# A recurrence, layer norms and a top-2 mixture of experts on one core: VectorE's order in the routing stage is rearranged, with TensorE's fillers and ScalarE's roots

## The chip, the cores and the metric

The kernel runs on one core of one Trainium2 chip. The metric is the device time of one execution in microseconds, lower is better. The kernel before takes 311.33 us (median of three runs, 310.96 to 311.38).

## What is computed

The input is 8 steps of 512 tokens with 128 features each. An LSTM runs over the 8 steps; its output is added to the input and normalised. Then the 4096 tokens go, in 8 groups of 512, through a mixture of 8 experts with two experts a token and 128 places an expert and group, and a second layer norm follows. Cut to what matters:

```python
def step(carry, xp_t):                       # x_proj = x @ w + bias, for 8 steps of 512 rows
    h_prev, c_prev = carry
    g = xp_t + h_prev @ u                    # [512, 4*128]
    gates = sigmoid(g[:, :3 * H]); c_cand = tanh(g[:, 3 * H:])
    c = fg * c_prev + ig * c_cand            # ig, fg, og = gates
    h = og * tanh(c)
    return (h, c), h
x = layernorm(x + lstm(x))
raw = softmax(einsum('GSM,ME->GSE', x, router_w))     # G = 8 groups of S = 512, E = 8
idx1 = argmax(raw); idx2 = argmax(raw without idx1)   # m1, m2: one hot; gate1, gate2
p1 = cumsum(m1) - m1;  p2 = cumsum(m2) - m2 + m1_count     # place in the expert; dropped if >= C = 128
expert_inputs = einsum('GSEC,GSM->EGCM', dispatch, x)
hidden = gelu(expert_inputs @ w0[e]) * (expert_inputs @ w1[e])     # 128 -> 680
out = einsum('EGCM,GSEC->GSM', hidden @ wo[e], combine)
x = layernorm(x + out)
```

## The kernel before

**Stages.** The loop over s (0 to 7) is the recurrence. Features lie on the partitions, 512 tokens in the columns. Products by w and by the experts' weights are made of three products of high and low parts (fp32r): ScalarE copies the high part, VectorE subtracts the low part (`low_x` for inputs, `low_weights` for a quarter of an expert, the low part of what follows). The h product is fp32. Behind the loop comes the expert stage: units u of one expert and two groups (later four), each with six chunks k; `first(u, k)` makes two products, ScalarE the gelu, VectorE `chunk` the product of both and `low_hid` its low part, and `second(u, k)` the output product three chunks later. The last stage is the second layer norm and the stores.

**One step s.** TensorE (L586 to L595): `h_part(s)` waits for h(s-1) and adds h @ u to four banks `big[0..3]`; `turn_sum(s-1)` transposes x + h into `b_ht` or `b_xnt`; `logits(s-1)` makes the router's products; `x_part(s+1)` fills the banks for the next step; `places(b)` counts for a batch b of two steps (`chosen` in, counts in `b_xt` out). ScalarE (L726 to L744): four Tanh of the gates, `exp(b)` of the softmax between gate 1 and gate 2, `norm_rows(s-2)` in two halves around the Tanh of the cell, then high parts by the lists `HIGH_X` and `HIGH_BY_ACT`. VectorE (L980 to L1031), in this order: `sum_y(s-1)` (x + h), `best(s-2)` (top two of the logits), `shift(s-2)` (the norm's offset, waits for GpSimd's root), `scale_less(b)` in odd steps; the first two parts of `assign_batch` in even steps; `term_f`; the softmax and the choice (`gate_step` 0 to 3) in odd steps, or the rest of `assign_batch` in even ones; `term_i`; `gate_step` 4 (`chosen`); the cell; `slot_base`; `stat(s-1)`; h; then moments and variance, `gate_values` and `gate_row` in odd steps, and `low_weights` by the list `LOW_BY_STEP`. The batch b = s // 2 - 1 is chosen in the odd step s, and its assignment (`slot_ix`, where each token's row goes) is made in the even step behind it.

**GpSimd** runs one queue in order (L479 to L489): `power(s)` is the norm's root x ** -0.5 of step s, and `scatter(b, ...)` issues two indirect DMAs for each of 8 tiles of 128 tokens, which write the normalised rows with their token number and gates to `slots`. It waits for `slot_step` (the assignment) and for `gate_rows_in`. Roots 3 to 7 stand among the scatters, ahead of the tile that `ROOTS_AMONG` names. `power(s)` also waits for the rows of step s-2. Behind the 64 scatters come the adds of the experts' output. **SyncE** loads and stores in order: `load_expert(e)` waits until the low parts of expert e-2 are made; `load_xd(u)` waits for the 16 scatters of its batches.

**Entering the expert stage.** `turn_xd(0)` transposes the first rows into `big[3]`, ScalarE and VectorE split them (`high_xd`, `low_xd`), and `first(0, 0)` starts. Batch 2's assignment, step 7's norm and batch 3's whole routing are still to do; VectorE does them between the chunks of units 0 to 3 (L1147 to L1193), among them `shift(S - 1)`, which waits for root 7, ahead of `chunk(0, 5)`.

**The last stage.** ScalarE copies the last outputs (`copy_y`, `last_y`), writes five early rows (`LATE_ROWS`), and then for each of two pairs of groups takes a square root (`fin_sqrt`, L812) and writes rows (L819). VectorE adds the last sums (`fin_add`, L1203), makes statistics (L1211), moments (L1215), the argument (L1221), and five small steps from the square root to scale and offset (`fin_root_step`, L1232 to L1241).

## Time and profile before

| | us |
|---|---|
| median of the runs (310.96 to 311.38) | 311.33 |
| the profiled execution's own time | 310.78 |
| its span, first to last instruction | 309.0 |
| busy in the span: TensorE, VectorE, ScalarE, GpSimd | 279.8, 257.9, 213.5, 176.7 |
| recurrence, until the last h product's start | 63.5 |
| first product of the expert stage | 74.0 |
| mean granted clock of TensorE | 0.979 of 2.4 GHz |

A row of a timeline gives the start in us, the duration, engine, line of the kernel, operation, what is written and read, its shape, how many instructions are merged in it, and in brackets the time for which the engine was idle before it, with what ended that. Instructions of one engine overlap a little, so in a full queue starts stand closer than durations.

### The profile page before, as it was taken

How to read it: one execution, taken by the hardware profiler on the slowest of the kernel's cores; microseconds unless marked ns; L12 is line 12 of the kernel's file. 1: busy time of each engine (PE TensorE's matmuls, PEld its weight loads, DVE VectorE, ACT ScalarE, POOL GpSimd, SP SyncE). 2: the span in 40 equal slices, each digit the busy share in tenths (PEclk: the TensorE clock that was granted, in tenths of full speed). 3: DMA queues.
4: the chain of work that ended last, by engine and by line, in shares of the span. 5: the costliest groups of instructions: out<-in, count | busy, mean ns of one | idle time of the engine just before them, and what ended most of it. 6: DMA issues, size and time to landing. Idle time of an engine off the chain costs nothing.

```text
span 309.0 us, 5728 instructions
## 1 busy us (share of the span) xinstructions
PE 279.8 (91%) x1671; PEld 233.7 (76%) x1671; DVE 257.9 (83%) x816; ACT 213.5 (69%) x484; POOL 176.7 (57%) x148
## 2 busy tenths in 40 slices
PE   8999988975969999999999999999999999897840
PEld 8666555635968999999998787788888888787730
DVE  2789997899859998888888988988777678899975
ACT  4787865556687777776778687776655665564964
POOL 5011148878777787776878578827447265662400
PEclk9999999977999999999999999999999999999995
DMA  6996081724273227224454857524223135452444
GB/s 193 379 395 238 8 253 48 217 69 134 78 225 92 71 69 228 65 57 52 72 93 35 204 71 164 71 20 64 45 25 45 26 34 146 67 94 19 79 143 136
DMA packets 46109, 34.97 MB, mean 113 GB/s; under 512 B 6993, under 2 KB 40720, under 8 KB 46080
## 3 DMA queue, kind: packets, MB, share of 16 engines
q1 hardware_dynamic: 35392, 26.56, 28.9%
q0 software_dynamic: 10688, 8.07, 17.8%
q8 instruction: 13, 0.21, 0.3%
q14 instruction: 16, 0.13, 0.1%
HBM read 17.86 MB, written 17.10 MB: 113 GB/s over the span
## 4 chain that ended last, share of the span: by engine, by line
PE 60%; DVE 15%; issue 8%; ACT 8%; POOL 8%; POOLq 0%; ACTq 0%; DVEq 0%
PE big L617 10%; PE big L619 10%; PE big L618 10%; POOL slots L464 6%; PE b_xnt L633 3%; PE b_xnt L636 3%; PE b_xnt L634 3%; PE big L531 2%; PE b_ht L633 2%; PE b_ht L636 2%; PE b_ht L634 2%; PE b_rt L653 2%; PE b_ht L578 2%; DVE e_lo L977 2%; PE b_xt L573 2%
## 5 line engine op out<-in xcount | busy, mean ns | idle before, releaser
L791 ACT ACTIVATE act_g<-big 128x256 f32<-128x256 f32 (+1 forms) x144 | 65.1, 452 | 55.4 <-PE big L619 54.6
L617 PE MATMUL big<-x_hi,e_hi 128*128 128x256 f32 (+1 forms) x264 | 84.7, 321 | 1.2 <-DVE x_lo L1037 1.2
L618 PE MATMUL big<-x_hi,e_lo 128*128 128x256 f32 (+1 forms) x264 | 84.4, 320 | 0.0
L619 PE MATMUL big<-x_lo,e_hi 128*128 128x256 f32 (+1 forms) x264 | 84.4, 320 | 0.0
L464 POOL DMA_INDIRECT slots<-rows,slot_ix x64 | 66.9, 1046 | 24.1 <-issue 18.4
L474 POOL DMA_INDIRECT tokens<-contrib,token_ix x32 | 50.3, 1572 | 32.0 <-DVE token_ix L1063 17.0
L474 POOL DMA_INDIRECT tokens<-zero_rows,token_ix x28 | 44.9, 1603 | 27.1 <-DVE token_ix L1063 20.0
L617 PEld LDWEIGHTS big<-x_hi,e_hi 128*128 128x128 f32 x264 | 50.2, 190 | 5.2 <-issue 1.5
L619 PEld LDWEIGHTS big<-x_lo,e_hi 128*128 128x128 f32 x264 | 50.3, 191 | 3.9
L618 PEld LDWEIGHTS big<-x_hi,e_lo 128*128 128x128 f32 x264 | 50.1, 190 | 3.9
L531 PE MATMUL big<-h,u_half 128*128 128x512 f32 x56 | 27.3, 633 | 3.5 <-DVE h L1018 3.5
L731 ACT ACTIVATE act_g<-big,bias_g 128x512 f32<-128x512 f32 x31 | 20.8, 685 | 8.1 <-PE big L531 7.7
L453 POOL TENSOR_TENSOR root_y<-root_x,minus_half 128x4 f32<-128x4 f32 x8 | 9.8, 1220 | 28.7 <-DVE root_x L882 28.7
L1071 DVE TENSOR_TENSOR term_i<-act_g,big 128x256 f32<-128x256 f32 (+3 forms) x36 | 18.3, 508 | 8.7 <-PE big L619 4.5
L1071 DVE TENSOR_TENSOR cell<-act_g,big 128x256 f32<-128x256 f32 (+1 forms) x36 | 18.3, 507 | 7.9 <-ACT act_g L791 4.4
L1071 DVE TENSOR_TENSOR h<-act_g,big 128x256 f32<-128x256 f32 (+3 forms) x36 | 18.3, 509 | 7.5 <-PE big L619 4.5
L531 PEld LDWEIGHTS big<-h,u_half 128*128 128x128 f32 x56 | 10.9, 200 | 16.7 <-issue 11.2
L977 DVE TENSOR_TENSOR e_lo<-e_raw,e_hi 128x544 fp32r<-128x544 f32 x32 | 22.6, 718 | 0.1
L1071 DVE TENSOR_TENSOR term_f<-act_g,big 128x256 f32<-128x256 f32 (+1 forms) x36 | 18.3, 507 | 5.1 <-PE big L619 2.9
L712 ACT ACTIVATE e_hi<-e_raw 128x544 fp32r<-128x544 f32 x32 | 20.1, 649 | 0.0
L756 ACT ACTIVATE hid_hi<-term_f 128x256 fp32r<-128x256 f32 (+1 forms) x36 | 17.3, 481 | 2.6 <-DVE term_f L1071 2.3
L756 ACT ACTIVATE h_hi<-h 128x256 fp32r<-128x256 f32 (+3 forms) x36 | 17.3, 481 | 1.6 <-DVE h L1071 1.5
(207 smaller groups left out, 654.1 us busy)
## 6 DMA issues: line engine op xcount, KB each, us to landing
e_raw<-in_L_ffn_w_kernel_dram SPq DMA_DIRECT2D x16, 320.0 KB
slots<-zero_rows SPq DMA_DIRECT2D x8, 548.0 KB, 8.4
e_raw<-in_L_ffn_wo_kernel_dram SPq DMA_DIRECT2D x8, 320.0 KB
xd<-slots SPq DMA_DIRECT2D x16, 137.0 KB, 2.5
xd<-slots SPq DMA_DIRECT2D x8, 274.0 KB, 3.1
x<-in_L_attn_input_seq_dram SPq DMA_DIRECT2D x8, 256.0 KB, 4.5
tokens<-rows SPq DMA_DIRECT2D x8, 256.0 KB, 2.7
x<-tokens SPq DMA_DIRECT2D x8, 256.0 KB, 3.2
```

What stands on the lines that cost most here:

```text
L464: pool.indirect_dma_start(slots, bass.IndirectOffsetOnAxis(ap=slot_ix[b][:, 2 * t + c:2 * t + c + 1], axis=0), rows[:, b * BT + t, :], Non ...
L474: pool.indirect_dma_start(tokens, bass.IndirectOffsetOnAxis(ap=tokens_of(u)[:, k:k + 1], axis=0), contrib(u)[:, k, :], None, bounds_check= ...
L531: pe.matmul(big[k][:, :], u_half[:, g * D:(g + 1) * D], h2[:, :], start=False, stop=True).then_inc(gate_ready, 1)
L617: pe.matmul(dst, e_hi[q][:, c0:c0 + m], xdt_hi[u % 2][:, 0:w], start=True, stop=False)
L618: pe.matmul(dst, e_lo[q][:, c0:c0 + m], xdt_hi[u % 2][:, 0:w], start=False, stop=False)
L619: mm = pe.matmul(dst, e_hi[q][:, c0:c0 + m], xdt_lo[u % 2][:, 0:w], start=False, stop=True)
L712: nc.scalar.activation(e_hi[e % RING_E][:, piece(n)], e_raw[e % 2][:, piece(n)], ACT.Copy).then_inc(ehi_ready[e % RING_E], 1)
L731: nc.scalar.activation(act_g[k][:, :], big[k][:, :], ACT.Tanh, bias=bias_g[:, gate_order[k]:gate_order[k] + 1], scale=1.0 if k == 2 else 0 ...
L756: nc.scalar.activation(hid_hi[n % RH][0:m, 0:width(u)], hid[n % RH][0:m, 0:width(u)], ACT.Copy).then_inc(hidhi_ready, 1)
L791: nc.scalar.activation(act0[n % RH][0:m, 0:w], pre(n, P)[0], ACT.Gelu_apprx_tanh).then_inc(gelu_ready, 1)
L977: dve.tensor_tensor(e_lo[e % RING_E][:, piece(n)], e_raw[e % 2][:, piece(n)], e_hi[e % RING_E][:, piece(n)], ALU.subtract).then_inc(elo_re ...
L1071: dve.tensor_tensor(hid[n % RH][0:m, 0:w], act0[n % RH][0:m, 0:w], pre(n, P)[1], ALU.mult).then_inc(hid_ready, 1)
```

## The change

VectorE makes `term_f` ahead of `shift` and `scale_less`, and `term_i` and the cell ahead of the whole softmax and choice (`gate_step` 0 to 4). Behind h, in the same odd step, it makes `void_base` (split off `gate_values`), all six parts of the batch's assignment, `gate_values` and `gate_row`; in the last step only `void_base`, since batch 2's assignment stays behind the loop, with its `gate_values` and `gate_row`. The low parts are spread anew: four quarters in step 2 (two of them ahead of `term_i`), one in step 3 (ahead), two in step 4, none in step 5, two in step 6; three of expert 2 come behind the loop instead of two. ScalarE makes `exp` behind all four gates and takes four high parts of expert 2 to other places, three of them ahead of `norm_rows`. Roots 5 to 7 move two scatters back on GpSimd. TensorE makes `logits(s-1)` in even steps between the halves of `x_part`, and dummy products (`keep_warm`) are added: ten behind step 6, twelve before `turn_xd(0)` and ten behind it. In the last stage ScalarE makes a dummy square root ahead of the last `copy_y`, the first real one comes after two of the five late rows, and VectorE makes its five steps of the first root ahead of `fin_add(0)`.

```diff
--- before.py
+++ after.py
@@ -48,9 +48,11 @@
     RING_E = 4
     HIGH_X = {0: [2, 3], 1: [4, 5], 2: [6, 7]}
     LOW_X = {0: [2, 3], 1: [4, 5], 2: [6, 7]}
-    HIGH_BY_ACT = {1: [(0, 0), (0, 1), (0, 2)], 2: [(0, 3), (1, 0)], 3: [(1, 1), (1, 2), (1, 3)], 4: [(2, 0), (2, 1)], 5: [(2, 2), (2, 3)]}
-    LOW_BY_STEP = {s: [((s - 2) // 2, 2 * (s % 2) + n) for n in range(2)] for s in range(2, 7)}
-    ROOTS_AMONG = {(0, 2): 3, (0, 5): 4, (0, 7): 5, (1, 2): 6, (1, 5): 7}
+    HIGH_BY_ACT = {1: [(0, 0), (0, 1), (0, 2)], 2: [(0, 3), (1, 0)], 3: [(1, 1), (1, 2), (1, 3)], 5: [(2, 2)]}
+    HIGH_AHEAD = {4: [(2, 0), (2, 1)], 6: [(2, 3)]}
+    LOW_AHEAD = {2: [(0, 0), (0, 1)], 3: [(1, 0)]}
+    LOW_BY_STEP = {2: [(0, 2), (0, 3)], 4: [(1, 1), (1, 2)], 6: [(1, 3), (2, 0)]}
+    ROOTS_AMONG = {(0, 2): 3, (0, 5): 4, (1, 0): 5, (1, 3): 6, (1, 6): 7}
     HIGH_AT = {3: [(3, 1), (3, 4), (4, 1), (4, 4)], 4: [(11, 4), (11, 5), (12, 2), (12, 3)], 5: [(12, 4), (12, 5), (13, 2), (13, 3)],
                6: [(13, 4), (13, 5), (14, 2), (14, 3)], 7: [(14, 4), (14, 5), (15, 2), (15, 3)]}
     LOAD_AT = {0: 4, 5: 5, 13: 6, 14: 7}
@@ -573,12 +575,12 @@
                     mm = pe.transpose(b_xd(u)[:, k * P:(k + 1) * P], xd[u % 4][:, k, 0:D], ident[:, :])
                 mm.then_inc(xdt_ready, 1)
 
-            def keep_warm(n):
+            def keep_warm(n, home):
                 for _ in range(n):
-                    pe.matmul(b_ht[:, 0:P], ones[:, :], ones[:, :], start=True, stop=True)
+                    pe.matmul(home[:, 0:P], ones[:, :], ones[:, :], start=True, stop=True)
 
             pe.wait_ge(pool_consts, 1)
-            keep_warm(12)
+            keep_warm(12, b_ht)
             x_part_0()
             router_sums()
             x_part(1, range(4))
@@ -586,14 +588,23 @@
             for s in range(1, S):
                 h_part(s)
                 turn_sum(s - 1)
-                logits(s - 1)
+                if s % 2 == 1:
+                    logits(s - 1)
                 if s + 1 < S:
                     x_part(s + 1, range(0, 2))
+                if s % 2 == 0:
+                    logits(s - 1)
+                if s + 1 < S:
+                    x_part(s + 1, range(2, 4))
                 if s >= 3 and s % 2 == 1:
                     places(s // 2 - 1)
-                if s + 1 < S:
-                    x_part(s + 1, range(2, 4))
+                if s == S - 2:
+                    pe.wait_ge(slot_step, AS * (GB - 1) + 2)
+                    keep_warm(10, b_xt)
+            pe.wait_ge(gate_read, gate_no(S - 1, 2))
+            keep_warm(12, big[2])
             turn_xd(0)
+            keep_warm(10, big[2])
 
 
             def first(u, k):
@@ -730,8 +741,10 @@
                     act.wait_ge(gate_ready, gate_no(s, k))
                     nc.scalar.activation(act_g[k][:, :], big[k][:, :], ACT.Tanh, bias=bias_g[:, gate_order[k]:gate_order[k] + 1],
                                          scale=1.0 if k == 2 else 0.5).then_inc(gate_read, 1)
-                    if k == 1 and s >= 3 and s % 2 == 1:
-                        exp(s // 2 - 1)
+                if s >= 3 and s % 2 == 1:
+                    exp(s // 2 - 1)
+                for e, n in HIGH_AHEAD.get(s, []):
+                    high_weights(e, n)
                 if s >= 2:
                     norm_rows(s - 2, range(0, 2))
                 act.wait_ge(cell_ready, s + 1)
@@ -803,6 +816,7 @@
                     for n in EARLY_ROWS.get((u - NU, k), []):
                         early_row(n)
             high_hid(NU - 1, NCH - 1)
+            nc.scalar.activation(root_p[:, 0, 0:1], eps[:, :], ACT.Sqrt)
             copy_y(NU - 1)
 
 
@@ -820,12 +834,16 @@
                                              bias=root_b[:, 1, n:n + 1], scale=root_y[:, 1, n:n + 1]).then_inc(fin_ready[g], 1)
 
             last_y()
-            for n in LATE_ROWS:
+            for n in LATE_ROWS[:2]:
                 early_row(n)
-            for i in range(NB // 2):
-                fin_sqrt(i)
-                for g in range(HALF + GB * i, HALF + GB * (i + 1)):
-                    fin_rows(g)
+            fin_sqrt(0)
+            for n in LATE_ROWS[2:]:
+                early_row(n)
+            for g in range(HALF, LAST):
+                fin_rows(g)
+            fin_sqrt(1)
+            for g in range(LAST, S):
+                fin_rows(g)
 
         @block.vector
         def _(dve):
@@ -936,10 +954,13 @@
                                          op0=ALU.mult, op1=ALU.add).then_inc(base_step, 1)
                 dve.tensor_scalar(void[:, :, :], gates[:, :, :], 0.0, FAR, ALU.is_equal, ALU.mult).then_inc(base_step, 1)
 
-            def gate_values(b):
+            def void_base(b):
 
                 dve.wait_ge(base_step, 3 * b + 2)
                 dve.tensor_tensor(base[:, :, :], base[:, :, :], void[:, :, :], ALU.add).then_inc(base_step, 1)
+
+            def gate_values(b):
+
                 dve.wait_ge(chosen_ready, b + 1)
                 dve.tensor_tensor(gate_rows[:, :, :, :], chosen[:, :, :, :], gates[:, :, :].unsqueeze(3).broadcast_to([P, BT, 2, E]),
                                   ALU.mult).then_inc(gates_step, 1)
@@ -978,39 +999,34 @@
                                   ALU.subtract).then_inc(elo_ready, 1)
 
             for s in range(S):
-                odd, even = (s // 2 - 1 if s % 2 == 1 and s >= 3 else None), (s // 2 - 2 if s % 2 == 0 and s >= 4 else None)
+                b = s // 2 - 1
+                routes = s >= 3 and s % 2 == 1
                 if s >= 1:
                     sum_y(s - 1)
                 if s >= 2:
                     best(s - 2)
-                    shift(s - 2)
-                if odd is not None:
-                    scale_less(odd)
-                if even is not None:
-                    assign_batch(even, 0)
-                    assign_batch(even, 1)
                 if s >= 1:
                     dve.wait_ge(gate_read, gate_no(s, 0))
                     dve.scalar_tensor_tensor(out=term_f[:, :], in0=act_g[0][:, :], scalar=1.0, in1=cell2[:, :],
                                              op0=ALU.add, op1=ALU.mult).then_inc(terms_ready, 1)
-                if odd is not None:
-                    for n in range(4):
-                        gate_step(odd, n)
-                if even is not None:
-                    for n in range(2, AS):
-                        assign_batch(even, n)
+                if s >= 2:
+                    shift(s - 2)
+                if routes:
+                    scale_less(b)
+                for e, n in LOW_AHEAD.get(s, []):
+                    low_weights(e, n)
                 dve.wait_ge(gate_read, gate_no(s, 2))
                 ins = dve.scalar_tensor_tensor(out=term_i[:, :] if s else cell2[:, :], in0=act_g[1][:, :], scalar=1.0,
                                                in1=act_g[2][:, :], op0=ALU.add, op1=ALU.mult)
                 ins.then_inc(terms_ready if s else cell_ready, 1)
-                if odd is not None:
-                    gate_step(odd, 4)
                 if s >= 1:
                     dve.wait_ge(terms_ready, 2 * s)
                     dve.scalar_tensor_tensor(out=cell2[:, :], in0=term_f[:, :], scalar=0.5, in1=term_i[:, :],
                                              op0=ALU.mult, op1=ALU.add).then_inc(cell_ready, 1)
-                if odd is not None:
-                    slot_base(odd)
+                if routes:
+                    for n in range(5):
+                        gate_step(b, n)
+                    slot_base(b)
                 if s >= 1:
                     stat(s - 1, range(T))
                 dve.wait_ge(tanh_ready, s + 1)
@@ -1024,9 +1040,13 @@
                 if s >= 1:
                     moment(s - 1)
                     variance(s - 1)
-                if odd is not None:
-                    gate_values(odd)
-                    gate_row(odd)
+                if routes:
+                    void_base(b)
+                    if s < S - 1:
+                        for n in range(AS):
+                            assign_batch(b, n)
+                        gate_values(b)
+                        gate_row(b)
                 for e, n in LOW_BY_STEP.get(s, []):
                     low_weights(e, n)
 
@@ -1150,11 +1170,13 @@
             assign_batch(NB - 2, 0)
             assign_batch(NB - 2, 1)
             shift(S - 2)
-            low_weights(2, 2)
+            gate_values(NB - 2)
+            gate_row(NB - 2)
+            low_weights(2, 1)
             chunk(0, 0)
             assign_batch(NB - 2, 2)
             chunk(0, 1)
-            low_weights(2, 3)
+            low_weights(2, 2)
             assign_batch(NB - 2, 3)
             stat(S - 1, range(0, 2))
             chunk(0, 2)
@@ -1167,6 +1189,7 @@
             assign_batch(NB - 2, 5)
             shift(S - 1)
             chunk(0, 5)
+            low_weights(2, 3)
             best(S - 1)
             for k in range(3):
                 chunk(1, k)
@@ -1181,6 +1204,7 @@
                 elif k == 3:
                     slot_base(NB - 1)
                 elif k == 4:
+                    void_base(NB - 1)
                     gate_values(NB - 1)
                 elif k == 5:
                     gate_row(NB - 1)
@@ -1258,13 +1282,12 @@
                 for t in range(T):
                     fin_moment(g * T + t)
             fin_argument(0)
+            for n in range(FT):
+                fin_root_step(0, n)
             for k in range(GB):
                 fin_add(k)
                 for t in range(T):
                     fin_stat(LAST + k, t)
-                if k == 0:
-                    for n in range(FT):
-                        fin_root_step(0, n)
             for n in range(LAST * T, S * T):
                 fin_moment(n)
             fin_argument(1)
```

## Rows read from the trace of the kernel before

**Rows 1.** The page, part 4: the chain that ended last, by engine.
```profile
PE 60%; DVE 15%; issue 8%; ACT 8%; POOL 8%; POOLq 0%; ACTq 0%; DVEq 0%
```
**Rows 2.** Windows: length, busy us of PE, PEld, DVE, ACT, POOL, then clock, DMA, GB/s.
```profile
64.00:66.00 2.00, 2.00 (x4) 0.75 (x3) 2.00 (x7) 0.69 (x1) 1.74 (x2) 0.50 0.56 166
...
120.00:128.00 8.00, 8.00 (x70) 7.96 (x70) 7.03 (x21) 5.71 (x18) 6.17 (x7) 1.00 0.41 123
```
**Rows 3.** Timeline of PE, the h products of steps 2, 3, 4 and 7.
```profile
18.84 3.60 PE L531 MATMUL big<-h,u_half 128*128 128x512 f32 x8
...
26.41 3.59 PE L531 MATMUL big<-h,u_half 128*128 128x512 f32 x8
...
35.08 3.70 PE L531 MATMUL big<-h,u_half 128*128 128x512 f32 x8 [0.22 <-DVE h L1018]
...
63.53 5.40 PE L531 MATMUL big<-h,u_half 128*128 128x512 f32 x8 [2.05 <-DVE h L1018]
```
**Rows 4.** Timeline of DVE, steps 3 and 4.
```profile
28.64 0.68 DVE L863 SCALAR_TENSOR_TENSOR yd<-h,x 128x512 f32<-128x512 f32 x1
...
34.35 0.67 DVE L1018 SCALAR_TENSOR_TENSOR h<-act_g,tanh_c 128x512 f32<-128x512 f32 x1
...
35.42 0.17 DVE L942 TENSOR_TENSOR base<-base,void 128x16 f32<-128x16 f32 x1
...
35.97 1.35 DVE L977 TENSOR_TENSOR e_lo<-e_raw,e_hi 128x544 fp32r<-128x544 f32 x2
...
39.00 0.17 DVE L950 TENSOR_SCALAR cnt<-b_xt 128x16 f32<-128x16 f32 x1
...
41.00 0.17 DVE L966 TENSOR_TENSOR slot_ix<-pos,over 128x16 uint32<-128x16 f32 x1
```
**Rows 5.** Timeline of POOL, scatters 1, 10 and 18, roots 5 and 7.
```profile
42.12 1.45 POOL L464 DMA_INDIRECT slots<-rows,slot_ix  x1 [5.46 <-DVE slot_ix L966]
...
56.39 0.97 POOL L464 DMA_INDIRECT slots<-rows,slot_ix  x1 [0.31 <-issue]
...
64.06 1.44 POOL L453 TENSOR_TENSOR root_y<-root_x,minus_half 128x4 f32<-128x4 f32 x1 [0.51 <-DVE root_x L882]
...
69.62 0.97 POOL L464 DMA_INDIRECT slots<-rows,slot_ix  x1 [0.30 <-issue]
...
82.47 1.04 POOL L453 TENSOR_TENSOR root_y<-root_x,minus_half 128x4 f32<-128x4 f32 x1 [0.40 <-DVE root_x L882]
```
**Rows 6.** Timelines of PE and DVE, entering the expert stage.
```profile
78.31 0.36 PE L617 MATMUL big<-x_hi,e_hi 128*128 128x256 f32 x1
...
83.55 0.16 DVE L888 SCALAR_TENSOR_TENSOR root_b<-moments,root_y 128x4 f32<-128x4 f32 x1 [0.24 <-POOL root_y L453]
...
86.64 0.36 PE L639 MATMUL b_ht<-hid_hi,e_lo 128*128 128x256 f32 x1 [0.99 <-DVE hid_hi L1045]
...
92.78 0.39 PE L633 MATMUL b_xnt<-hid_hi,e_hi 128*128 128x256 f32 x1 [1.54 <-ACT hid_hi L756]
```
**Rows 7.** Timelines of ACT and DVE, the last stage.
```profile
294.79 0.38 ACT L762 ACTIVATE tanh_c<-b_xnt 128x256 f32<-128x256 f32 x1 [1.40 <-PE b_xnt L640]
...
297.30 0.76 DVE L1203 TENSOR_TENSOR x<-b_rt,x 128x256 f32<-128x256 f32 x2 [0.90 <-PE b_rt L666]
...
298.07 1.28 ACT L812 ACT_TABLE_LOAD   x1
...
299.70 0.20 DVE L1232 RECIPROCAL root_y<-root_p 128x8 f32<-128x8 f32 x1 [0.87 <-ACT root_p L812]
...
300.63 0.75 DVE L1203 TENSOR_TENSOR x<-b_ht,x 128x256 f32<-128x256 f32 x2
...
300.74 2.80 ACT L819 ACTIVATE x<-x,root_b,root_y 128x128 f32<-128x128 f32 x7 [1.08 <-DVE root_b L1241]
...
302.74 0.17 DVE L1221 TENSOR_SCALAR root_x<-fin_mom 128x8 f32<-128x8 f32 x1
...
303.45 0.29 ACT L812 ACTIVATE root_p<-fin_mom,eps 128x8 f32<-128x8 f32 x1
```

## The prediction

> **What bounds the kernel now.** Read the shares of the chain first [rows 1]: TensorE owns 60% of the chain that ended last, VectorE 15%, GpSimd and ScalarE 8% each, and 8% is issue, most of it GpSimd's. So there are stages in which another engine sets the pace. Then the windows [rows 2]: from about 112 to 256 us TensorE has no gap (the window from 120 is 8.00 of 8.00), so whatever moves the start of this stage moves the end by as much, and nothing inside it is touched. What counts lies ahead of it and behind it.
>
> Ahead of it the timelines show a recurrence of eight steps. A step whose h product starts at 18.84 and whose successor starts at 26.41 costs TensorE 7.57 us of its own work; the next takes 8.67 us, to 35.08, and there TensorE waits for h [rows 3]. VectorE explains it: from sum_y(2) at 28.64 to h(3) at 34.35 it runs without a gap, and the assignment of batch 0, cnt at 39.00 to slot_ix at 41.00, stands in the next step with a gate term of 0.60 between its parts [rows 4]. GpSimd waits 5.46 us for that slot_ix, starts at 42.12 and is then full: a scatter takes 0.97 us and 0.30 us of issue, and root 7, behind 26 scatters and four roots, starts at 82.47 [rows 5]. VectorE waits for root 7 at 83.55 (0.24 us), and what it does next releases TensorE at 86.64, after 0.99 us idle [rows 6]. The chain of waits runs through just these: POOL from 43.87 on, root 7, VectorE, the product at 86.64. So the first half is bound by GpSimd's start, by the number of scatters ahead of root 7, and by what VectorE does between shift(7) and low_hid(0,5).
>
> At the end the last ScalarE table load stands at 298.07, VectorE waits 0.87 us for its root, and the second root waits at 303.45 until ScalarE has written seven rows, though VectorE had its argument at 302.74 [rows 7].
>
> **Part 1, steps 2 and 3: later h, earlier slots.** A low part costs 0.64 us (two in 1.35 us with their overlap, row 35.97 of [rows 4]; one more in a queue adds 0.64). Step 2 gets four in place of two. The two more can cost VectorE between 0 and 1.27 us; since one pair stands ahead of term_i, where VectorE waits for the third gate, I take 0.54. h(2) ends later by as much, while TensorE is in its own work until 26.4: hidden. But VectorE enters step 3 at 29.18 instead of 28.64. Step 3 to h took 5.71 us (28.64 to 34.35); it gets one low part more (0.64) and two waits of some 0.12 us each where a result is used at once, since chosen no longer fills the wait ahead of the cell. h(3) starts at 29.18 + 5.71 + 0.64 + 0.25 = 35.78 instead of 34.35, and h product 4 at 36.5 instead of 35.1: **this step loses 1.4 us**, TensorE idle for about 1.3 of it. From h to void_base it takes 1.07 us as before (34.35 to 35.42): 36.85, with the add itself 36.94. Then the assignment: 39.00 to 41.17 less 0.60 for the gate term is 1.57, and 0.10 for a wait that the term used to cover. slot_ix is there at 38.6 instead of 41.17. The gate rows now follow it (35.51 to 35.97: 0.46 us, end 39.1), and GpSimd waits for them too. From slot_ix's end to the first scatter the trace has 0.95 us [rows 4, 5]; so GpSimd starts at 40.0, **2.1 us earlier**. Bounds: 39.5 if the delay counts from slot_ix alone, 41.0 if VectorE pays the whole 1.27 in step 2 and waits a little more in step 3.
>
> **Part 2, GpSimd up to root 7.** The roots move from (0,7), (1,2), (1,5) to (1,0), (1,3), (1,6): root 7 stands behind 28 scatters, not 26. The sum: 82.47, less the start's 2.1, less the waits of 0.51 (root 5) and 0.40 (root 7) for VectorE's arguments, which come in time now, plus 2 x 1.28 = 2.57: **82.0 instead of 82.47**. Four roots stay four. Argument 7 is made behind chunk (0,3), at about 81.2, and so doesn't hold it. Ten scatters with root 3 among them, 42.12 to 56.39, take 14.27 us; eight slots of 1.28 and one of 2.23 with the root would be 12.47, so 1.8 us of lengthening lie there (the first takes 1.45 instead of 0.97) [rows 5]. I leave it where it is. Without it root 7 would be at 81.2 (its argument), with twice it at 83.8.
>
> **Part 3, steps 4 to 7.** Step 4 has no assignment in it any more and is TensorE's 7.6 us; the two copies ahead of the rows on ScalarE (1.2 us) delay tanh, but h still ends inside TensorE's work. Step 5 has VectorE's assignment behind h and not two low parts, which is hidden or even, and root 3, 2.1 us earlier, is no longer waited for; I take 8.3 us. Step 6 is again TensorE's, 7.6, but ten dummies follow: the h product's four products are 8 pieces of 512 columns in 3.59 us, so a dummy of 128 columns, two pieces, is 0.21 us, and ten are 2.1 [rows 3]. So the last h product starts at 62.3, not 63.53. Before, TensorE had idled 2.05 us ahead of it, the granted clock was 0.50 from 64 to 66 (the level of 1.2 GHz), and the product took 5.40 instead of 3.6 [rows 2, 3]. Now the dummies fill that gap; I expect 3.6. Then it waits from about 67.0 to 68.4 for chosen(2) (shift(5), ahead of scale_less, waits some 1 us for root 5, which two more scatters put at 64.0 to 65.4), then 12 dummies (2.6), the turn of xd (whose rows are no longer waited for: their last scatter is 4 us earlier), 10 dummies (2.1): first(0,0) at 73.9, and at 2.4 GHz first(0,2) at 76.4 instead of 78.31 [rows 6]: 1.9 us earlier. VectorE, with 0.46 us of gate rows more ahead of its first chunk and 0.2 of pieces, comes to shift(7) at 82.1 instead of 83.31 and **waits there for root 7 until 83.1**. The 1.9 us end here, and 1.0 us of slack is left for all of this part: it is free unless it slips by more.
>
> **Part 4, behind root 7.** shift(7) is 0.45 us earlier. Low part (2,3) now stands between chunk (0,5) and best(7): +0.64, less about 0.3 of small waits that vanish, since everything is ready. The product of 86.64, which waits for low_hid(0,5), comes **0.15 us earlier**. The wait of 1.54 us at 92.78 [rows 6] follows the same chain (copy, exp's two table loads), so it moves along. Scatters of batches 1 to 3 end about 2.7 us earlier, which nobody waits for.
>
> **Part 5, the tail.** ScalarE idles 1.40 us until 294.79 [rows 7]. The dummy root with its table load (1.28, row 298.07) and about 0.2 goes there: 293.39 + 1.48 = 294.87, so 0.1 us late. Three of the five early rows, at 0.40 each (seven in 2.80), go behind sqrt(0): it starts at 296.95 and is done at 297.25. VectorE's five steps (299.70 to 300.63) follow at once and push fin_add(0) from 297.30 to 298.2. From there the old spacing without the steps between: add and stats 0, 1.47 us (297.30 to 298.77), add and stats 1 with eight moments 2.11 (300.63 to 302.74): sqrt(1) at 301.8. ScalarE's three early rows and seven rows (2.80) end at 301.2, ahead of it. Before it was 303.45: **1.65 us earlier**, and all behind it is unchanged. If the joined order hid nothing but the table load, it would be 1.3; if the 0.1 is also absorbed, 1.8.
>
> ScalarE's page of the Trainium skill (ScalarE: Activation LUTs, What ACT_TABLE_LOAD costs) says a switch costs about 1.28 us of load and 1.38 us of drain. That speaks against the dummy root: it wouldn't fit into the idle time. The row of 298.07 with 1.28 and VectorE released at 299.70 by the root behind it leaves no room for such a drain, so I weigh it as a rival only.
>
> **Sum.** -0.15 and -1.65 make -1.8 us: a span of 307.2 instead of 309.0, and a profiled run of 309.0 instead of 310.78. The profiled run is 0.55 us below the median of 311.33, so I predict 309.5.
>
> **Rivals.**
> (a) GpSimd's slow slots vanish, since expert 2's load no longer runs with them: root 7 at 81.2, 0.8 us more in the middle, 308.7. For: the lengthening is in the first ten. Against: later ones occur without that load. 0.10.
> (b) TensorE's clock falls in step 7's wait for chosen(2). Idle 1.54 us ahead of 92.78 left it, 2.05 ahead of 63.53 did not; I have 1.45. Then the twelve dummies take twice 2.6, as the product took 5.40 for 3.6, first(0,0) comes at 76.6, VectorE at 84.8, and 1.7 us of the gain go: 311.2. 0.11.
> (c) Slower: the price of the two scatters put ahead of root 7. If the slow slots belong to scatters and not to that time, each of the 28 takes 0.18 us more (1.8 in ten), 5.0 in all instead of 1.8: root 7 at 85.2, VectorE waits for it until 86.3, which is 2.7 later than 83.55, +0.3 for the low part behind it, -1.65 for the tail: +1.35, 312.7. It decides from a root 7 at about 84.0 on. Against: the slots from 65 to 82 are nearly all 1.28. 0.18, into which I count a GpSimd start that slips.
> (d) The dummy root doesn't fit into ScalarE's idle time. If the switch takes twice its 1.28 us there, copy_y is at 293.39 + 2.76 = 296.15, 1.35 late, last rows and sums too, fin_add(0) is held by its sum until 298.65 and ScalarE's rows shift; of the tail's gain 0.3 is left: 310.9. For: no row shows a load in a queue that has just drained. Against: 298.07. 0.05. By the page named above the same edit would come out about so.
>
> The forecast itself has 0.56, and its own range is 308.9 to 310.5. A measurement of this kernel can tell about 0.2%, 0.6 us, from no change. Faster: forecast and (a), 0.66. Within: (b) and (d), 0.16. Slower: (c), 0.18. The range of 8 in 10 takes in (a), (b) and (d) and leaves (c) out: 308.1 to 311.6.
>
> **What would show it.** h product 4 at 36.5; the first scatter at 40.0; no wait for root 3; a last h product of 3.6 us with clock 1.00 from 64 to 70; first(0,2) near 76.4; then VectorE's wait of about 1 us for root 7, at 83.1; the product of 86.64 at 86.5; sqrt(1) 1.65 us earlier against the last turn of y. The prediction is wrong if root 7 isn't waited for (then the middle gains up to 1.9), if the first scatter isn't before 41, or if the clock is below 1.00 anywhere between 60 and 90.

## The result and the profile after

The changed kernel takes 310.75 us (median of 16 runs, 310.11 to 312.25), the kernel before 311.73 beside it (16 runs, 310.96 to 313.67). The ratio is 0.9965, with a 95% interval of 0.9948 to 0.9981: about 1.0 us faster (0.6 to 1.6), where 1.8 were forecast. The profiled execution took 310.11 us, the lowest of the 16 times, with a span of 308.4 (before 310.78 and 309.0).

**Reading the two traces against each other.** TensorE's third h product (step 2) starts at 17.95 in this execution and at 18.84 in [rows 3], though nothing ahead of it was changed. Over the executions below, of all kernels, this start lies anywhere between 17.95 and 19.31. So within the first half I count from this h product and write **h+** for it: before, the product that waits for low_hid(0,5) (86.64 in [rows 6]) is at h+67.80. It is called the product with chunk 5 below. shift(s) is VectorE's row that writes `root_b` (L888 before, L906 after).

The last stretch first, ScalarE's timeline of the kernel after (start us, us, engine, line, op, out<-in, count, [idle before <-releaser]):

```profile
294.46 1.28 ACT L819 ACT_TABLE_LOAD   x1
295.76 0.20 ACT L819 ACTIVATE root_p<-eps 128x1 f32<-128x1 f32 x1
295.87 0.37 ACT L775 ACTIVATE tanh_c<-b_xnt 128x256 f32<-128x256 f32 x1
...
297.86 0.29 ACT L826 ACTIVATE root_p<-fin_mom,eps 128x8 f32<-128x8 f32 x1
...
302.76 0.30 ACT L826 ACTIVATE root_p<-fin_mom,eps 128x8 f32<-128x8 f32 x1 [0.74 <-DVE fin_mom L1239]
```

and TensorE's last turn of y, the transposition of the last output:

```profile
296.29 0.44 PE L664 MATMUL b_xt<-ident,tanh_c 128*128 128x128 f32 x2 [0.48 <-ACT tanh_c L775]
```

The table load lies where ScalarE had been idle, and sqrt(1) waits for VectorE now, not the reverse. From the last turn of y to sqrt(1) it is 6.47 us (302.76 - 296.29). Before, the turn stood at 295.23 and sqrt(1) at 303.45 [rows 7]: 8.22. **The tail gave 1.75 us**, where I had 1.65.

Now the first half. TensorE's timeline after:

```profile
35.51 3.70 PE L533 MATMUL big<-h,u_half 128*128 128x512 f32 x8 [1.13 <-DVE h L1034]
...
59.26 2.39 PE L580 MATMUL b_xt<-ones 128*128 128x128 f32 x20
61.49 3.60 PE L533 MATMUL big<-h,u_half 128*128 128x512 f32 x8
...
68.72 0.20 PE L557 MATMUL b_xt<-chosen,before 128*128 128x64 bf16 x1 [2.39 <-DVE chosen L948]
...
69.04 4.49 PE L580 MATMUL big<-ones 128*128 128x128 f32 x24
...
75.74 0.37 PE L628 MATMUL big<-x_hi,e_hi 128*128 128x256 f32 x1
...
87.79 0.36 PE L650 MATMUL b_ht<-hid_hi,e_lo 128*128 128x256 f32 x1 [1.63 <-DVE hid_hi L1065]
```

Windows of the same trace (columns as in [rows 2]; the third number from the end is the granted clock):

```profile
68.00:70.00 2.00, 1.28 (x14) 1.29 (x15) 1.93 (x10) 0.91 (x3) 1.39 (x2) 0.73 0.46 103
70.00:72.00 2.00, 2.00 (x12) 2.00 (x11) 1.35 (x8) 0.00 (x0) 1.69 (x2) 0.50 0.96 260
...
120.00:128.00 8.00, 8.00 (x69) 7.96 (x69) 6.98 (x20) 5.95 (x19) 6.07 (x7) 1.00 0.48 143
```

The reader should see four things. The last h product takes 3.60 us in place of 5.40: the dummies ahead of it do what they are for. TensorE then waits 2.39 us for chosen(2), its clock goes to 0.50 (1.2 GHz), and the 24 dummy pieces take 4.49 us. The product that low_hid(0,5) releases is at 87.79, 1.15 **later** than before, or 2.04 later when counted from the h product (h+69.84). And from 120 on TensorE is as full as it was, so this delay goes to the end: the last turn of y is 1.06 later (296.29 against 295.23), or 1.95 counted from the h product.

GpSimd's timeline after, scatter 1, a slow scatter, roots 5 and 7:

```profile
39.08 1.20 POOL L466 DMA_INDIRECT slots<-rows,slot_ix  x1 [2.04 <-DVE rows L993]
...
47.42 1.52 POOL L466 DMA_INDIRECT slots<-rows,slot_ix  x1 [0.30 <-issue]
...
64.83 1.05 POOL L455 TENSOR_TENSOR root_y<-root_x,minus_half 128x4 f32<-128x4 f32 x1
...
82.98 1.04 POOL L455 TENSOR_TENSOR root_y<-root_x,minus_half 128x4 f32<-128x4 f32 x1
```

and VectorE's:

```profile
65.92 0.16 DVE L906 SCALAR_TENSOR_TENSOR root_b<-moments,root_y 128x4 f32<-128x4 f32 x1 [1.95 <-POOL root_y L455]
...
74.20 0.42 DVE L1057 TENSOR_TENSOR x_lo<-big,x_hi 128x256 fp32r<-128x256 f32 x1 [2.81 <-ACT x_hi L763]
...
82.47 0.42 DVE L900 TENSOR_SCALAR root_x<-moments 128x4 f32<-128x4 f32 x1
...
84.06 0.16 DVE L906 SCALAR_TENSOR_TENSOR root_b<-moments,root_y 128x4 f32<-128x4 f32 x1 [0.50 <-POOL root_y L455]
...
84.93 0.71 DVE L998 TENSOR_TENSOR e_lo<-e_raw,e_hi 128x544 fp32r<-128x544 f32 x1
```

Root 5 starts only at 64.83, VectorE waits 1.95 us for it in shift(5), and chosen(2), behind that on VectorE, is late. Then VectorE comes to shift(7) at 83.56, not at 82.1, and waits another 0.50 for root 7. Root 7 itself is held by two things at once: its argument (82.47) ends at 82.89, and the last scatter ahead of it at 82.90. So the theory: **the tail gave all of the gain, and the middle lost a part of it, by late roots (5, then 7) and by the low part (2,3)**.

In most sets of runs below every kernel, the one before included, took 355 to 362 us in place of 311, with ScalarE held for up to 12.7 us at a time between some 68 and 170 us (shown at the end), so I read those by their ratios and by what lies ahead of the first such stop, and the traces at about 309 us carry the sums.

### The profile page after: what moved, and what is told of

Its sections match the earlier page's. It is cut to its first block, busy times and chain, and to the rows that moved or that the text cites. A ratio compares the mean times of both kernels' runs of the same rounds, so it can differ in the third digit from the quotient of the medians.

```text
span 308.4 us, 5858 instructions
## 1 busy us (share of the span) xinstructions
PE 283.7 (92%) x1735; PEld 239.9 (78%) x1735; DVE 258.2 (84%) x816; ACT 214.1 (69%) x485; POOL 179.6 (58%) x148
## 4 chain that ended last, share of the span: by engine, by line
PE 54%; DVE 21%; issue 10%; POOL 8%; ACT 6%; POOLq 0%; ACTq 0%; DVEq 0%
PE big L628 10%; PE big L630 10%; PE big L629 10%; POOL slots L466 7%; PE b_xnt L644 3%; PE b_xnt L647 3%; PE b_xnt L645 2%; DVE e_lo L998 2%; PE b_ht L647 2%; PE b_rt L664 2%; PE b_ht L644 2%; DVE hid_lo L1065 2%; PE b_ht L645 2%; PE b_xt L575 1%; PE b_ht L580 1%
## 5 line engine op out<-in xcount | busy, mean ns | idle before, releaser
L466 POOL DMA_INDIRECT slots<-rows,slot_ix x64 | 69.0, 1078 | 20.7 <-issue 18.4
L476 POOL DMA_INDIRECT tokens<-contrib,token_ix x32 | 51.1, 1596 | 28.9 <-DVE token_ix L1083 17.6
L742 ACT ACTIVATE act_g<-big,bias_g 128x512 f32<-128x512 f32 x31 | 21.1, 687 | 12.7 <-PE big L533 12.3
L533 PE MATMUL big<-h,u_half 128*128 128x512 f32 x56 | 25.5, 598 | 1.4 <-DVE h L1034 1.4
L769 ACT ACTIVATE hid_hi<-cell 128x256 fp32r<-128x256 f32 (+1 forms) x36 | 17.3, 481 | 2.2 <-DVE cell L1091 2.1
```

Of the source, the lines that this page charges most:

```text
L466: pool.indirect_dma_start(slots, bass.IndirectOffsetOnAxis(ap=slot_ix[b][:, 2 * t + c:2 * t + c + 1], axis=0), rows[:, b * BT + t, :], Non ...
L476: pool.indirect_dma_start(tokens, bass.IndirectOffsetOnAxis(ap=tokens_of(u)[:, k:k + 1], axis=0), contrib(u)[:, k, :], None, bounds_check= ...
L533: pe.matmul(big[k][:, :], u_half[:, g * D:(g + 1) * D], h2[:, :], start=False, stop=True).then_inc(gate_ready, 1)
L742: nc.scalar.activation(act_g[k][:, :], big[k][:, :], ACT.Tanh, bias=bias_g[:, gate_order[k]:gate_order[k] + 1], scale=1.0 if k == 2 else 0 ...
L769: nc.scalar.activation(hid_hi[n % RH][0:m, 0:width(u)], hid[n % RH][0:m, 0:width(u)], ACT.Copy).then_inc(hidhi_ready, 1)
```

## The experiments

In those sets the kernel before had 360.25 us in the first set (35 runs), 359.52 in the second (29), 360.71 in the fourth (23), 360.37 (17), and 356.48 in the last (17).

### The tail alone, and the change without its tail

The first is the kernel before with this, and the second the kernel after with the same undone:

```diff
             high_hid(NU - 1, NCH - 1)
+            nc.scalar.activation(root_p[:, 0, 0:1], eps[:, :], ACT.Sqrt)
             copy_y(NU - 1)
...
-            for n in LATE_ROWS:
+            for n in LATE_ROWS[:2]:
                 early_row(n)
+            fin_sqrt(0)
+            for n in LATE_ROWS[2:]:
+                early_row(n)
...
             fin_argument(0)
+            for n in range(FT):
+                fin_root_step(0, n)
             for k in range(GB):
                 fin_add(k)
...
```

> The kernel before with the last stage of the changed kernel alone (dummy square root ahead of the last copy_y, first root after two late rows, its five steps ahead of fin_add(0)). Theory A, the tail gains by itself what its profile shows (1.75 us from the last turn of y to the second square root) and the middle gives 1.1 back: 1.7 us less than before, ratio 0.9945. Rival B, the tail's gain needs the earlier arrival of other work or is lost in the last stores: less than 0.5 us, ratio above 0.998. The last turn of y stays at 295.2, the second square root comes at 301.7.

Measured: 358.86 us, ratio 0.9974 (0.9932 to 1.0015). The interval holds both forecasts.

> The changed kernel with the last stage of before. Theory A: slower than before by what the middle lost, 1.1 us in the profile, ratio 1.003 to 1.004; the product behind low_hid(0,5) at 87.8 as in the changed kernel. Rival B: the middle is neutral in the median and the profile's 1.1 us was chance: ratio within 0.001 of 1.

Measured: 362.07 us, ratio 1.0071 (1.0040 to 1.0103). Without its tail the change is slower than the kernel before, by 1.4 to 3.7 us. The 2.04 us above lie in that.

> The kernel before with the change's tail alone. Theory A (the tail gave 1.75 us and the middle lost 1.1): 1.6 to 1.8 us under the kernel before, ratio 0.994 to 0.995, so better than the whole change. Rival B (the two traces differ by chance, the tail gives 1 us and the middle nothing): ratio 0.9965 to 0.997, as the whole change.

Measured: 358.37 us, ratio 0.9983 (0.9958 to 1.0007).

> The kernel before with the change's tail alone, beside a kernel before of 311.8 us. Theory A (the tail gave 1.75 us and the middle lost 1.1): ratio 0.994 to 0.995. Rival B (the tail gives about 1 us and the middle nothing): 0.9965 to 0.997. Measured at about 360 us the same kernel gave 0.9974 and 0.9983, with intervals of 0.004 to either side.

Measured: 356.62 us, ratio 0.9896 (0.9854 to 0.9938). The three ratios of one kernel spread by more than their intervals; they can't size the tail. In the last of their traces the last h product took 3.70 us behind the usual wait, where the other four executions of the kernel before and of the tail alone have 5.32 to 5.40:

```profile
63.03 3.70 PE L531 MATMUL big<-h,u_half 128*128 128x512 f32 x8 [2.05 <-issue]
```

So the clock doesn't always fall in a wait of 2.05 us either: the window from 64 to 66 has 1.00 here and 0.50 in [rows 2]. An undisturbed execution can size the tail:

> The kernel before with the change's tail alone; one look at the trace. Theory A: from the last turn of y to the second square root 6.4 to 6.6 us instead of 8.2, everything ahead of it as in the kernel before, span 307.2 to 307.5 if its start has the phase of the kernel before (309.0).

Measured: 309.28 us, span 307.5, beside a kernel before of 312.68. TensorE's timeline and ScalarE's second root:

```profile
86.84 0.36 PE L639 MATMUL b_ht<-hid_hi,e_lo 128*128 128x256 f32 x1 [0.99 <-DVE hid_hi L1050]
...
295.45 0.44 PE L653 MATMUL b_xt<-ident,tanh_c 128*128 128x128 f32 x2 [0.49 <-ACT tanh_c L762]
```

```profile
301.93 0.30 ACT L813 ACTIVATE root_p<-fin_mom,eps 128x8 f32<-128x8 f32 x1 [0.74 <-DVE fin_mom L1220]
```

Its third h product is at 19.01, so the product of 86.84 is at h+67.83, as before (67.80), and from the last turn of y to sqrt(1) it is 6.48 us. The tail is worth 1.74 us by itself (8.22 less 6.48) and touches nothing else; the span from the third h product on is 288.5 us here and 290.2 before (309.0 - 18.84). By the same count the whole change has 290.45, so by these traces the tail alone is the better kernel. The ratios taken in one set point the same way (0.9983 against 1.0014 for the whole change), but their intervals overlap.

### The change unaltered, beside the others

> The changed kernel itself, unaltered, as the yardstick of the three beside it. Both theories expect its ratio of 0.9965 to the kernel before again (0.995 to 0.998), its wait of 2 to 2.5 us for the choice of batch 2 in step 7 and a granted clock under 1.00 between 68 and 72 us, and products of the second layer with chunk 5 of group 0 at about 87.8 us. If this chip is disturbed like the last one, its ratio is the number against which the others are read.

Measured: 359.56 us, ratio 1.0014 (0.9986 to 1.0042), so no gain in this condition. Step 7 repeats: chosen at h+50.74 (h+50.77 in the first trace), first product at h+58.57 (57.79).

### The roots back

```diff
-    ROOTS_AMONG = {(0, 2): 3, (0, 5): 4, (1, 0): 5, (1, 3): 6, (1, 6): 7}
+    ROOTS_AMONG = {(0, 2): 3, (0, 5): 4, (0, 7): 5, (1, 2): 6, (1, 5): 7}
```

> The changed kernel with roots 5, 6 and 7 at their old places among the scatters, (0,7), (1,2), (1,5). Theory A, the two scatters put ahead of roots 5 to 7 make step 7 wait (1.95 us on VectorE, 2.39 on TensorE, then clock 0.50): root 5 comes 2.6 us earlier, shift(5) waits for at most 0.2, TensorE waits under 1 us for chosen(2), the dummies run at 2.4 GHz, first(0,0) comes some 3.5 us earlier than 75.7, shift(7) at about 82 and the product of 87.79 at about 85.9: 1.9 us faster than the changed kernel, ratio 0.991 against before. Rival C, what counts is the low part that stands behind shift(7) and argument 7: no more than 0.5 us of gain, ratio 0.995 or above.

Measured: 356.56 us, ratio 0.9920 (0.9887 to 0.9952), below rival C's 0.995. Root 5 came 2.87 us earlier (h+44.01 against 46.88), but TensorE still waited 1.25 us for chosen(2), not under 1.

> The changed kernel with the roots of batches 5 to 7 back behind as many scatters as before (26 instead of 28 ahead of root 7). Theory A (the middle lost its gain because the lengthened slots of the scatters made roots 5 and 7 late, and step 7's wait for the choice dropped the clock): root 5 at about 63.3 and no wait of the shift for it, clock 1.00 through step 7, first product of the first layer at 74.4 or earlier instead of 75.7, VectorE at shift(7) no longer waits for root 7; time 1.5 to 2.5 us under the changed kernel, ratio 0.989 to 0.992. Rival B (the low part spread anew and VectorE's own work set the middle, the roots are cover): within 0.7 us of the changed kernel, ratio 0.995 to 0.9965.

Measured: 357.31 us, ratio 0.9953 (0.9925 to 0.9981).

> The changed kernel with the roots of batches 5 to 7 back behind as many scatters as before, here beside a kernel before of 311.8 us. Theory A (the late roots and the clock that step 7's wait dropped took the middle's gain, 1.1 to 1.3 us): 1 to 2 us under the changed kernel, ratio 0.990 to 0.9935 to the kernel before; clock 1.00 through step 7; products of the second layer with chunk 5 of group 0 at 86.9 or earlier for an h product of step 7 that starts at 62.0. Rival B (the low part spread anew sets the middle): ratio 0.995 to 0.9975.

Measured: 358.09 us, ratio 0.9936 (0.9895 to 0.9977).

> The changed kernel with the roots of batches 5 to 7 back behind as many scatters as before. Theory A (late roots and the clock that step 7's wait dropped took the middle's gain): 1 to 2 us under the changed kernel, ratio 0.990 to 0.9935 to the kernel before; clock 1.00 through step 7. Rival B (the low part spread anew sets the middle): ratio 0.995 to 0.9975. If the kernel before takes some 360 us again, the ratio is read only with the earlier ones.

Measured: 357.81 us, ratio 0.9950 (0.9917 to 0.9982). All four ratios lie below the change's 1.0014; in the second set, beside the change itself, the difference is 2.2 us and the intervals don't overlap. Step 7 of the first of them, TensorE's timeline and a window:

```profile
68.89 0.20 PE L557 MATMUL b_xt<-chosen,before 128*128 128x64 bf16 x1 [1.25 <-DVE chosen L948]
...
69.17 2.92 PE L580 MATMUL big<-ones 128*128 128x128 f32 x24
...
74.43 0.36 PE L628 MATMUL big<-x_hi,e_hi 128*128 128x256 f32 x1
```

```profile
68.00:72.00 4.00, 3.11 (x35) 3.11 (x36) 3.42 (x18) 1.20 (x3) 3.08 (x4) 1.00 0.46 112
```

TensorE waits 1.25 us, the clock stays at 1.00 (2.4 GHz), the 24 pieces take 2.92 us in place of 4.49, and the first product is at h+55.19 in place of 57.79. That is what I had forecast (h+55.06). The wait for root 5 is gone. An undisturbed execution:

> Roots of batches 5 to 7 back behind as many scatters as before; one look at the trace. Theory A: clock 1.00 from 60 to 76 us; from the start of the h product of step 7 to the first product of the first layer 11.6 us instead of the changed kernel's 14.3, to the products of the second layer with chunk 5 of group 0 at most 25.0 instead of 26.3; span 306.5 to 307.5. Rival B: to the products with chunk 5 26.0 or more, span 308 or more.

Measured: 309.52 us, span 307.8. TensorE:

```profile
68.29 0.20 PE L557 MATMUL b_xt<-chosen,before 128*128 128x64 bf16 x1 [1.33 <-DVE chosen L948]
...
68.57 4.48 PE L580 MATMUL big<-ones 128*128 128x128 f32 x24
...
75.33 0.37 PE L628 MATMUL big<-x_hi,e_hi 128*128 128x256 f32 x1
...
87.12 0.36 PE L650 MATMUL b_ht<-hid_hi,e_lo 128*128 128x256 f32 x1 [1.61 <-DVE hid_hi L1065]
```

GpSimd and VectorE:

```profile
82.32 1.04 POOL L455 TENSOR_TENSOR root_y<-root_x,minus_half 128x4 f32<-128x4 f32 x1 [1.74 <-DVE root_x L900]
```

```profile
83.39 0.17 DVE L906 SCALAR_TENSOR_TENSOR root_b<-moments,root_y 128x4 f32<-128x4 f32 x1 [0.24 <-POOL root_y L455]
...
84.27 0.71 DVE L998 TENSOR_TENSOR e_lo<-e_raw,e_hi 128x544 fp32r<-128x544 f32 x1
```

This expectation was half wrong. The product with chunk 5 is at h+68.51 (third h product 18.61), 1.33 us earlier than in the change, as expected, and the span of 307.8 lies between the two forecasts. But the clock fell here too, after a wait of only 1.33 us, and the first product is at h+56.72. So a wait of 1.25 to 1.33 us went both ways: in seven executions of kernels with the roots back and the dummies of step 6 in place, five kept the clock (waits of 1.25 to 1.31 us, first product at h+55.07 to 55.19) and two did not (1.25 and 1.33 us; 56.67, 56.72), while with the roots as changed all four executions waited longer and fell (2.0 to 2.4 us; first product at 57.64 to 58.92). Root 7 is now held by its argument and no more by scatters, and shift(7) is at h+64.78, as in the kernel before (64.71). What is left of the loss, 68.51 against 67.80, is 0.71 us. The low part behind shift(7), 84.27, takes 0.64 of it: from shift(7) to the product with chunk 5 it is 3.09 us before and 3.73 here and in the change. This holds in every trace, disturbed or not: 3.72 to 3.74 in the nine with the low part at this place, 3.09 to 3.11 in the eleven without it, among them one that differs from the change in nothing but this place (the first of the next section). **So the 2.04 us split into 1.33 for the late roots, 0.64 for the low part, and 0.07 that I give to neither.** The clock had fallen in both of these executions. Where it didn't, the first product is another 1.5 us earlier; what that is worth at the product with chunk 5 no undisturbed trace shows.

> Root 5 alone back where it was, 6 and 7 as in the change. Theory A (argument and scatters hold root 7 equally, at 82.89 and 82.90 in the changed kernel, so neither root alone brings anything): step 7's shift does not wait for root 5, argument 7 is up to 1.2 us earlier, but root 7 still starts 64.8 to 65.1 us behind the h product of step 2 and the products with chunk 5 come at 69.5 to 69.9. Rival B (root 5's delay of step 7 is the whole cause): root 7 at 64.0, products with chunk 5 at 68.6.

Only (0, 7): 5 put back. Measured: 359.19 us beside 357.39. ScalarE:

```profile
79.79 0.38 ACT L763 ACTIVATE x_hi<-big 128x256 fp32r<-128x256 f32 x1 [11.02 <-remote]
```

The stop fell into the very stretch that was to be read. chosen is at h+49.67 (50.77 in the change), so root 5 was indeed what held it; but whether root 5 or root 7 holds the product with chunk 5 isn't answered. GpSimd went on through the stop and had the 28 scatters ahead of root 7 done at h+63.82, against h+64.95 in the changed kernel's trace. So what root 5 alone would bring depends on the slow scatters of the execution, and lies between nothing and 1.1 us of the 1.33; this is argued, not shown.

### The low part (2,3) elsewhere

```diff
             chunk(0, 5)
-            low_weights(2, 3)
             best(S - 1)
...
             scale_less(NB - 1)
+            low_weights(2, 3)
             for k in range(3, NCH):
```

> The changed kernel with low part (2,3) not between chunk (0,5) and best(7) but ahead of chunk (1,3), behind scale_less(3), where VectorE idles 2.84 us during ScalarE's table loads. Theory A and rival C agree on its price: the product of 87.79 comes 0.6 us earlier and so does everything behind it, ratio 0.9945 against before. Rival D, the part only moves to where TensorE waits for it (first(2,0) needs all four low parts): no gain, ratio 0.9965.

Measured: 359.76 us, ratio 1.0011 (0.9973 to 1.0049), as the change has without the edit (1.0014). The 0.64 us are gone from their place (3.11 us from shift(7) to the product with chunk 5), and the time doesn't show it.

> The roots back, and the low part (2,3) behind the scaling of the scores of batch 3, where VectorE is less pressed. Theory A (with the roots in place the 0.64 us of the low part still lie on VectorE's way to the products of the second layer with chunk 5): another 0.3 to 0.6 us under the kernel with the roots back alone, ratio 0.987 to 0.991. Rival B (at its new place it is late for the products of batch 1 with expert 3, or lies on the same way): within 0.2 us of the kernel with the roots back, or slower.

Measured: 356.22 us, ratio 0.9912 (0.9881 to 0.9943).

> The roots back, and the low part (2,3) behind the scaling of the scores of batch 3. Theory A (the low part's 0.64 us lie on VectorE's way to the products with chunk 5): 0.3 to 0.6 us under the kernel with the roots back alone, ratio 0.988 to 0.992; the low part itself starts after 89 us. Rival B (it lies on the same way at its new place): within 0.2 us of the kernel with the roots back.

Measured: 357.74 us, ratio 0.9932 (0.9895 to 0.9968), against 0.9953 and 0.9936 for the roots back alone in the same sets: the intervals overlap. Both have 3.09 us from shift(7) to the product with chunk 5. The next trace shows where the gain can go.

### Without the added dummies

The kernel of the last section with the roots back, and:

```diff
-                    keep_warm(10, b_xt)
...
-            keep_warm(12, big[2])
             turn_xd(0)
-            keep_warm(10, big[2])
```

> The kernel with the roots back and the low part (2,3) later, without the change's 32 added dummy products (the waits ahead of them stay). Theory A (the dummies hold the clock in the two waits of step 7, as they are meant to): without them the granted clock falls below 0.8 somewhere between 60 and 76 us, the last h products take over 4 us instead of 3.6 or the first products of the first layer run at half the clock, and the products of the second layer with chunk 5 of group 0 are 0.5 us or more later than with them. Rival B (they only fill idle time, and since they stand in TensorE's queue ahead of the first products they cost up to 0.2 us): the first product starts at 74.2 or earlier at full clock and nothing is late.

Measured: 309.81 us, span 308.1, beside 311.83. TensorE and a window:

```profile
66.91 0.20 PE L557 MATMUL b_xt<-chosen,before 128*128 128x64 bf16 x1 [1.70 <-DVE chosen L946]
...
72.73 0.55 PE L626 MATMUL big<-x_hi,e_hi 128*128 128x256 f32 x1 [1.02 <-DVE x_lo L1055]
...
87.03 0.36 PE L648 MATMUL b_ht<-hid_hi,e_lo 128*128 128x256 f32 x1 [0.94 <-DVE hid_hi L1063]
...
97.64 0.44 PE L575 MATMUL b_xt<-ident,xd 128*128 128x128 f32 x2 [0.60 <-DMA xd<-slots]
```

```profile
72.00:76.00 4.00, 3.27 (x15) 3.30 (x16) 3.58 (x23) 2.83 (x7) 3.20 (x4) 0.50 0.35 117
```

Both theories have a part. The dummies hold the clock: without them it is 0.50 from 68 to 80. But the ten of step 6 cost what they take: the last h product starts at h+41.44 without them and at h+43.5 with them, and takes 3.67 us all the same. Here it needs no warming, since it no longer waits: VectorE's new order had ended that wait. And first products at 1.2 GHz from h+53.86 on bring root 7 (h+64.00) only 0.29 us later than with the dummies (63.71, in an execution whose clock fell too). The product with chunk 5, with the low part now behind it, is at h+68.16, 0.35 us earlier than with the roots back alone. But nothing of it is left: TensorE's last gap of this stretch ends at h+91.85, in the kernel with the roots back at h+91.82, in the kernel before at h+91.15. It goes in the wait of 0.60 us at 97.64 for the next rows, which the kernel with the roots back doesn't have: SyncE's load of them waits for scatters behind root 7 and is issued at h+76.27 in place of 75.91. So the 32 dummies together changed nothing at the end of this stretch in these two executions, and what the low part costs at its new place isn't shown.

### All causes taken away

The roots back, the ten dummies of step 6 out, and three low parts of expert 2 in VectorE's gap ahead of low_xd(0) (2.81 us at 74.20) in place of their old places:

```diff
+            for n in range(1, 4):
+                low_weights(2, n)
             low_xd(0)
...
```

> Roots 5 to 7 back; low parts (2,1), (2,2) and (2,3) directly ahead of the low part of the first unit's x, where VectorE sat idle for 2.6 to 2.8 us; the ten dummies of step 6 left out. Counted from the h product of step 2, the kernel before has the products of the second layer with chunk 5 of group 0 at 67.8, the changed one at 69.8, the one with the roots back at 68.5. Theory A (VectorE's own work is the way to them, 0.64 us for each low part, and the dummies of step 6 only delay): h product of step 7 at 41.4, first product of the first layer at 54.7, products with chunk 5 at 66.3 to 67.0, span 305.3 to 306.8. Rival B (another engine, or root 7 behind its scatters, is right behind VectorE): 67.4 or later, span 307 or more.

Measured: 355.31 us beside 357.39.

> The same kernel once more, timed. Beside a kernel before of 311.8 us: Theory A (1.3 us for the roots, 0.6 us for the low part in front of the products with chunk 5, up to 1.3 us for the two others): 306.5 to 308.5 us, ratio 0.983 to 0.990, products of the second layer with chunk 5 of group 0 66.3 to 67.0 us behind the h product of step 2. Rival B (the next engine is right behind VectorE): 308.7 to 309.6 us, ratio 0.990 to 0.993, as the tail alone or the roots back. Beside a kernel before of about 360 us: A 0.986 to 0.991, B 0.992 to 0.995.

Measured: 355.63 us, ratio 0.9964 (0.9933 to 0.9996). VectorE of the first:

```profile
69.77 1.99 DVE L998 TENSOR_TENSOR e_lo<-e_raw,e_hi 128x544 fp32r<-128x544 f32 x3
73.45 0.42 DVE L1057 TENSOR_TENSOR x_lo<-big,x_hi 128x256 fp32r<-128x256 f32 x1 [1.70 <-ACT x_hi L763]
```

The three fit and leave 1.70 us idle; first products come at h+55.08 and 55.16. Behind this both executions are disturbed. The gain of theory A is not in the ratio (its 0.991 lies outside the interval), nor is it refuted for an undisturbed execution: this kernel has none.

## Why the prediction was wrong in size

The direction was right, and 310.75 lies in the range, but 1.8 us were forecast and 1.0 came. The direction is the tail's; the middle was forecast as a small gain and was a loss, so that the time still lies in the range is luck in part.

- **Part 1 held.** h product 4 at h+17.56 (forecast 17.66), step 3 10.0 us long (10.1), first scatter at h+21.13 (21.16).
- **Part 2 failed, and it is the step that matters.** From the first scatter to root 7 I had 42.0 us, with 1.8 of slow slots left in their old place. It took 43.90 (39.08 to 82.98). Scatters of 1.3 to 1.5 us of busy time, slots of 1.6 to 1.8, now occur over the whole stretch up to 79 us, where I had left the lengthening in the first ten scatters (which are nine slots, not ten as I counted). That is rival (c)'s mechanism, which I had sized at 5.0 us of lengthening in all; against the 40.2 us that my sum has without it, it came to 3.7. It differs between executions: four others with 28 scatters ahead of root 7, all of them disturbed, had these done 41.9 to 43.4 us behind the first one's start, this one 43.8. Root 7 is at h+65.0 instead of 63.2, and root 5 at h+46.9, beyond the later end of what I had given it (65.4, so h+46.6). Argument 7, which I had at 81.2 (h+62.4), was late as well, at h+64.52, by what part 3 lost.
- **Part 3 failed by that root.** The last h product took 3.6 us as forecast, at h+43.54 (43.46). But shift(5) waited 1.95 us for root 5, not 1, and chosen(2) made TensorE wait 2.39 us, not 1.45. Then the clock fell: **rival (b) happened**, first product at h+57.8 and not 55.1, just where that rival puts it (76.6, so h+57.8), and VectorE's slack of 1.0 us was used up: it came to shift(7) at h+65.6 and not at 63.3. The text had named a clock below 1.00 between 60 and 90 as a sign that it was wrong. The roots put back gave 55.1 to 55.2 in five of seven executions. Even my 1.45 would not have been safe: 1.33 once was too much, and 1.25 once. The row I had gone by, 1.54 us idle at 92.78 with the clock held [rows 6], has another surrounding: full work ahead of it.
- **Part 4 failed with its low part.** I took 0.3 us off its 0.64 for small waits. Nothing came off: 3.73 us from shift(7) to the product in place of 3.09. And shift(7) itself, forecast 0.45 us earlier, came 1.40 later by parts 2 and 3 (h+66.11 against 64.71).
- **Part 5 held**, 1.75 against 1.65: the 0.1 us that the dummy root was to cost copy_y didn't come (TensorE's last turn follows the product ahead of it by 0.77 us, 295.52 to 296.29, before by 0.76). The drain of 1.38 us that the Trainium skill's page "ScalarE: Activation LUTs" names (What ACT_TABLE_LOAD costs) isn't there: load at 294.46, root at 295.76, 1.30 us later, copy at 295.87. Rival (d) fell.

So the step that failed is GpSimd's queue up to roots 5 and 7, with the wait for chosen(2) that it lengthened and the clock that fell in it. The middle came to +2.04 in place of -0.15, and the tail to -1.75: +0.3 by the traces from the third h product on, against -1.8. The spans differ by -0.6 and the medians of 16 by -1.0. The span's share of the rest is the start, 0.9 us early in the one profiled execution. That the medians still show 1.0 stays open by about 1.3 us: the traces are single executions, and the kernel before varies by 2.7 us over its runs. Not tried one by one are exp behind all four gates, ScalarE's high parts, and the new place of the logits; what they do together is in the step times of parts 1 and 3, which held up to step 7.

## What to carry to other kernels

When work is added to a queue that is already full, charge each piece with the queue's measured mean slot, slow ones included, and not with its nominal one; then follow every reader of what stands behind it, not only the last (root 5 delayed chosen(2) before root 7 was even due). Dummies ahead of a product pay only while that product would wait anyway; once another part of the change ends the wait, they are a delay of their own length. And a change in two places should be tried in halves: here the small half was the better kernel by its undisturbed trace.

## What was not expected of the hardware

The start of a program varies: its third h product, behind identical work, is at 17.95 to 19.31 us in the 20 traces.

A whole set can run 45 to 50 us long at the same program. Three rows of ScalarE and one of TensorE in the change unaltered, 359.56 us:

```profile
104.98 1.28 ACT L804 ACT_TABLE_LOAD   x1 [5.78 <-remote]
...
119.90 0.38 ACT L804 ACTIVATE act_g<-big 128x256 f32<-128x256 f32 x1 [8.54 <-remote]
...
159.38 0.38 ACT L804 ACTIVATE act_g<-big 128x256 f32<-128x256 f32 x1 [9.24 <-remote]
```

```profile
107.02 0.58 PE L644 MATMUL b_xnt<-hid_hi,e_hi 128*128 128x256 f32 x1 [7.32 <-issue]
```

TensorE's products ahead had ended at 99.7, and ScalarE took up its next work 5 us later; GpSimd went on scattering meanwhile. Tail alone and roots back show the same stops in the same stretches (ScalarE at 119.06 after 11.33 us, at 117.70 after 6.51), and three executions on other occasions had none. I didn't find what holds ScalarE. It may change a ratio, where a stop swallows a gain made ahead of it; that is not shown.
